# First attention of a two-layer model: four projections in one run, q and k six blocks ahead, scores a step early, running sums in float32r

## The chip, the cores and the metric

One core of one Trainium2 chip runs the whole program. The metric is device microseconds (us) from launch to end; lower is better. PE is TensorE, DVE VectorE, ACT ScalarE, POOL GpSimd, SP the queue that issues most DMAs.

## What is computed

The input is 64 sequences of 32 tokens with 256 features. Two layers follow, each of a conditioned linear map, an attention, a second conditioned map and a feed-forward net. The change touches only the first attention (16 heads, key and value width 128, 64 slots per head):

```python
q = _rope(hs @ Wq.T); k = _rope(hs @ Wk.T); v = hs @ Wv.T
s = clip(hs @ Ws1.T @ Ws2.T + bs2, -32, 32)
z = cumlogsumexp(s, over tokens); es = exp(s); enz = exp(-z)
A  = where(mask, q @ k.T * scale, 0)
ok = enz * (A @ es);  qv = softmax(ok, axis=-1)
W2 = where(mask, (qv * enz) @ es.T, 0)
o  = W2 @ v
o_n = o * rsqrt(mean(o*o) + EPS) * g_norm_weight
x  = x + (o_n * silu(hs @ Wg.T)) @ Wo.T
```

## The kernel before

`attention0` works in 64 steps. A step `i` is one block of 128 tokens (four sequences) and four heads; 16 blocks make a pass, and the four passes take the four groups of heads. `hs` and the projection weights are split in a high and a low float32r part, so each projection is six matmuls of 512 columns (two halves of the features, three products).

Each engine has its own program, written out by hand, and waits on semaphores. In a step, PE does:

- `x1(i)` and `x2(i)`: the two halves of a quarter of q or k (`quarter`), always over four blocks at once, so that four steps fill the q and k of the next four blocks. DVE multiplies each result by cosine and sine (`x1_by_cos`, `x1_by_sin`, `x2_by_both`), and POOL's `rotate` adds them.
- `proj_v(i+1)` into PSUM bank PJ0, which ACT's `v_out` copies out, and `proj_g(i+1)` into bank PJ1, which ACT's `g_t` (tanh) and DVE's `silu` read. `x1` and `x2` use the same two banks: `x1` waits for `v_out`, `x2` for `silu`.
- `slots(i+1)`: the slot logits, one float32r matmul; DVE's `clip`, then ACT's `s_e` makes `es`. `running(i+1)` multiplies `es` with a triangle of ones (float32, two passes) for the sums over tokens; DVE's `z` takes reciprocals (`enz`).
- `scores(i)` and `slot_scores(i)`, 32-wide tiles, with DVE's mask `am` between; then DVE's `ok` and its minimum `mn`, ACT's four exponentials `ex`, POOL's `exz`, and `turn_p(i)`, a transpose.
- `slot_weights(i)`, tiled; DVE's mask `wm`; `values(i-1)`, tiled; ACT's `square`, DVE's `norm_sum` and `gated`, POOL's `norm` (`rstd`, then `og`); `turn_og(i-1)`, transposes; ACT's `ogT_out`; `heads_out(i-2)`, four float32 matmuls (eight passes in the records); DVE's `y_out` adds to `xres`.

POOL also makes the low half of the next weights (`split`). The last four steps have no `x1` and `x2`. The file then goes on to stages that the change leaves alone.

Of the kernel before, what the change touches and what calls it, by code (L numbers as in the profile page):

```python
# [38 lines left out]
def attention0(nc, k, xres, x, cond, wcond, w_slices, wo, ws1, ws2b, ucol, gnorm, rope_cos, rope_sin, maskA, mask01, mask01_own):  # L39

    with ExitStack() as ctx:
# [23 lines left out]
        cosb = sb("cosb", [P, TOK])  # L65
        sinb = sb("sinb", [P, TOK])
# [13 lines left out]
        es = sb("es", [P, SW])  # L80
        enz = sb("enz", [P, SW])
# [16 lines left out]
        ogT_s = sb("ogT_s", [P, QW])  # L98
# [12 lines left out]
        products = [(t1c[:, :], t1s[:, :], t2c[:, :], t2s[:, :]), (gs[:, 1, :], og[:, :], sq[:, :], ogT_s[:, :])]  # L111
# [26 lines left out]
        TURNS = QUAD * (STEPS // QUAD)  # L138

# [20 lines left out]
        s_clip, s_exp, z_rec = sem("s_clip"), sem("s_exp"), sem("z_rec")  # L160
        a_mm, a_mask = sem("a_mm"), sem("a_mask")
# [44 lines left out]
        def _(pool):  # L206
# [37 lines left out]
            for j in range(QUAD):  # L244
                rotate(j)
# [11 lines left out]
            for i in range(STEPS):  # L257
                if i >= 1:
                    norm(i - 1)
                pool.wait_ge(ok_exp, HQ * (i + 1))  # L260
                pool.wait_ge(pT_tr, i)
                pool.tensor_tensor(exz[:, :], ex[:, :], enz[:, :], ALU.mult).then_inc(p_z, 1)
                if QUAD + i < TURNS:
                    rotate(QUAD + i)
                if LEAD + i < STEPS:
# [5 lines left out]
            norm(LAST)  # L271

        @block.tensor
        def _(pe):
# [51 lines left out]
            def x2(i, part):  # L326
                j = QUAD + i
                if j < TURNS:
                    if part.start == 0:
                        pe.wait_ge(g_silu, i + 1)  # L330
                    quarter(j, 1, x2_mm, part)

            def proj_v(i, part):
                if part.start == 0:
                    pe.wait_ge(x1_sin, min(QUAD + i, TURNS))
                    pe.wait_ge(v_ev, i)
                    pe.wait_ge(w_second, i // G * G + 1)
# [44 lines left out]
            def slot_scores(i):  # L382
                pe.wait_ge(a_mask, i + 1)
                pe.wait_ge(ok_z, i)
                for h in range(HQ):
# [11 lines left out]
            def heads_out(i):  # L397

                pe.wait_ge(ogT_ev, i + 1)
                pe.wait_ge(a_mask, min(i + 3, STEPS))  # L400
                pe.wait_ge(wo_scaled, i // G + 1)
                for h in range(HQ):
                    m = pe.matmul(AW[:, 2 * P:2 * P + D], ogT_s[:, h * P:(h + 1) * P], w_o[:, i // G % 2, h, :],  # L403
                                  start=(h == 0), stop=(h == HQ - 1))
                m.then_inc(y_mm, 1)
# [5 lines left out]
            def slot_weights(i):  # L411
                pe.wait_ge(pT_ev, i + 1)
                pe.wait_ge(esT_ev, i + 1)
                pe.wait_ge(y_add, i - 1) if i >= 2 else None
# [28 lines left out]
            for j in range(2, QUAD):  # L443
# [7 lines left out]
            proj_v(0, A)  # L451
            proj_g(0, A)
            pe.wait_ge(ld, 16 * LOADS)
            running(0)
            turn_es(0)
            for i in range(STEPS):
                more = i < LAST
                if i >= 1:
# [26 lines left out]
        def _(act):  # L485
# [53 lines left out]
            v_out(0)  # L539
            g_t(0)  # L540
            esT_out(0)
            split(G)
            def square(i):
# [4 lines left out]
            def ogT_out(i):  # L548
                act.wait_ge(y_mm, i)
                copy(ogT_s[:, :], TB[:, :], ogT_tr, i + 1, ogT_ev)  # L550

            for i in range(STEPS):
                more = i < LAST
                if i >= 1:
                    square(i - 1)
                if LEAD + i < STEPS:
                    split(LEAD + i)
# [6 lines left out]
                if more:  # L564
                    s_e(i + 1)
                act.wait_ge(w2_mm, i)
                copy(pT_s[:, :], TA[:, 0:SW], pT_tr, i + 1, pT_ev)
                if i >= 1:
                    ogT_out(i - 1)
                if more:  # L570
                    v_out(i + 1)
                    esT_out(i + 1)
                    g_t(i + 1)
            square(LAST)
# [3 lines left out]
        def _(dve):  # L578
# [20 lines left out]

            def x1_by_cos(j):  # L600
                dve.wait_ge(x1_mm, j + 1)
                dve.wait_ge(qk_add, j if j >= QUAD else max(j - 1, 0))
                dve.tensor_tensor(products_of(j)[0][:, :], banks_of(j)[0][:, :], cosb[:, :], ALU.mult).then_inc(x1_cos, 1)

            def x1_by_sin(j):
                dve.tensor_tensor(products_of(j)[1][:, :], banks_of(j)[0][:, :], sinb[:, :], ALU.mult).then_inc(x1_sin, 1)

            def x2_by_both(j):
                dve.wait_ge(x2_mm, j + 1)
                dve.tensor_tensor(products_of(j)[2][:, :], banks_of(j)[1][:, :], cosb[:, :], ALU.mult).then_inc(x2_cos, 1)  # L610
# [43 lines left out]
            for j in range(QUAD):  # L654
# [9 lines left out]
            for i in range(STEPS):  # L664
                j, more = QUAD + i, i < LAST
                silu(i)
                if i >= 1:
                    gated(i - 1)
                dve.wait_ge(a_mm, i + 1)
                dve.wait_ge(ok_mm, i)  # L670
                dve.tensor_tensor(by_pairs(am), both, for_heads(mA), ALU.mult).then_inc(a_mask, 1)
                if i >= 1:
                    norm_sum(i - 1)
                dve.wait_ge(ok_mm, i + 1)
                dve.wait_ge(z_rec, 2 * i + 2)
                dve.wait_ge(ok_exp, HQ * i)
                dve.scalar_tensor_tensor(out=ok[:, :], in0=OE[:, 0:SW], scalar=-1.0, in1=enz[:, :],
                                         op0=ALU.mult, op1=ALU.mult).then_inc(ok_z, 1)
                dve.wait_ge(ok_z, i + 1)
                dve.tensor_reduce(mn[:, :], heads(ok[:, :]), AX.X, ALU.min).then_inc(ok_min, 1)  # L680
                if more:
                    clip(i + 1)
# [3 lines left out]
                if i >= 2:  # L686
                    y_out(i - 2)
                dve.wait_ge(ok_exp, HQ * (i + 1))
                dve.tensor_reduce(sm[:, :], heads(ex[:, :]), AX.X, ALU.add).then_inc(p_sum, 1)
                dve.wait_ge(p_sum, i + 1)  # L690
                dve.scalar_tensor_tensor(out=sme[:, :], in0=sm[:, :], scalar=RMS_EPS, in1=sm[:, :],
                                         op0=ALU.mult, op1=ALU.mult).then_inc(p_eps, 1)
                if j < TURNS:
                    x2_by_both(j)
                if more:
                    z(i + 1, 0)
                    z(i + 1, 1)
                dve.wait_ge(w2_mm, i + 1)
                dve.wait_ge(o_mm, i)
# [1371 lines left out]
```

## Time and profile before

| | |
|---|---|
| median of three runs | 1491.48 us (1489.26 to 1494.16) |
| the profiled execution, its own time | 1494.37 us |
| its span, first to last instruction | 1492.5 us |
| busy: PE, DVE, ACT, POOL | 1361.8, 918.0, 507.1, 514.6 us |
| first attention, first to last mask `wm` | 67.0 to 805.7 us |
| the same, number of steps | 64 |
| mean granted TensorE clock | 0.968 |

The span is the profiled execution's own; the profiler's times of matmuls are modelled at their end, so a matmul's cost in a stream is read from the distance between two starts, not from its length.

### The profile page before, as it was taken

To read this page: it belongs to the slowest core of one execution; us is meant where nothing else is said; L and a number is where in the kernel's file an instruction comes from. 1 tells how busy PE (TensorE), PEld (TensorE's weight loads), DVE (VectorE), ACT (ScalarE), POOL (GpSimd) and SP (SyncE) were. 2 spreads that over 40 slices of the span, in tenths; PEclk is the share of its full clock that TensorE was granted. 3 is DMA by queue.
4 is the path that set the end of the run, shared out by engine and by line. 5 is a ranking of instruction groups with operands and counts; after the bars stand their busy time and mean duration, and the time that the engine had idled before them with its cause. 6 is when DMAs were issued, how large, how long until landed. Compare 5 with 4: busy or idle time off the path is not lost. (4 is left out here: it accounts for less than half of the span.)

```text
span 1492.5 us, 46698 instructions
## 1 busy us (share of the span) xinstructions
PE 1361.8 (91%) x19926; PEld 1060.2 (71%) x19926; DVE 918.0 (62%) x1825; ACT 507.1 (34%) x1123; POOL 514.6 (34%) x544
## 2 busy tenths in 40 slices
PE   2999999999999999999996598999999689997996
PEld 2677777777777777777764486777777567775664
DVE  2777777777777777777764465242433335665886
ACT  2344443444443444333342313132322222222332
POOL 0655545555544555544432212221212111122111
PEclk9999999999999999999999699999999879997998
DMA  6000000000001000000000510000000540000620
GB/s 200 9 13 13 14 16 13 27 13 13 13 16 28 13 13 13 3 2 3 2 2 2 201 52 1 0 0 0 0 1 0 167 121 1 0 0 3 197 66 22
DMA packets 33414, 47.57 MB, mean 32 GB/s; under 512 B 6718, under 2 KB 22296, under 8 KB 32728
## 3 DMA queue, kind: packets, MB, share of 16 engines
q1 hardware_dynamic: 31048, 42.69, 9.2%
q8 instruction: 133, 2.18, 0.6%
q10 hardware_dynamic: 2112, 2.10, 0.5%
q14 instruction: 41, 0.34, 0.1%
q0 software_dynamic: 80, 0.26, 0.1%
HBM read 42.68 MB, written 2.36 MB: 30 GB/s over the span
## 5 line engine op out<-in xcount | busy, mean ns | idle before, releaser
L233 POOL TENSOR_TENSOR rstd<-mse,mhalf 128x4 f32<-128x4 f32 x64 | 65.1, 1017 | 238.5 <-DVE mse L651 238.5
L563 ACT ACTIVATE ex<-ok,mn 128x64 f32<-128x64 f32 x256 | 68.2, 337 | 193.7 <-DVE mn L680 193.7
L403 PE MATMUL AW_TA<-w_o,ogT_s 128*128 128x256 f32 x512 | 129.0, 395 | 0.7 <-ACT ogT_s L488 0.7
L822 POOL TENSOR_TENSOR hT_lo<-h,hT_hi 128x512 fp32r<-128x512 f32 x44 | 56.8, 1292 | 192.8 <-ACT hT_hi L995 192.8
L228 POOL TENSOR_TENSOR turned<-t1c,t2s 128x512 f32<-128x512 f32 x62 | 79.8, 1287 | 117.5 <-DVE t2s L611 117.5
L626 DVE SCALAR_TENSOR_TENSOR gs<-gs,PJ 128x512 f32<-128x512 f32 x64 | 44.0, 687 | 122.5 <-ACT gs L504 122.5
L622 DVE RECIPROCAL enz<-SC 128x128 f32<-128x128 f32 x128 | 112.6, 921 | 4.7 <-PE SC L354 4.7
L303 PE MATMUL PJ<-hs_hi,w_hi 128*128 128x512 f32 x248 | 115.2, 464 | 0.0
L1058 DVE SCALAR_TENSOR_TENSOR t<-th,m 128x512 f32<-128x512 f32 (+1 forms) x56 | 38.4, 685 | 121.3 <-ACT th L1000 93.5
L314 PE MATMUL PJ<-w_hi,hs_hi 128*128 128x512 f32 x256 | 111.7, 436 | 0.0
L403 PEld LDWEIGHTS AW_TA<-w_o,ogT_s 128*128 128x128 f32 x512 | 93.0, 191 | 17.2 <-ACT ogT_s L488 1.0
L314 PE MATMUL PJ<-w_hi,hs_lo 128*128 128x512 f32 x256 | 100.2, 391 | 0.0
L314 PE MATMUL PJ<-w_lo,hs_hi 128*128 128x512 f32 x256 | 100.0, 391 | 0.0
L303 PE MATMUL PJ<-hs_hi,w_lo 128*128 128x512 f32 x248 | 98.2, 396 | 0.0
L303 PE MATMUL PJ<-hs_lo,w_hi 128*128 128x512 f32 x248 | 96.8, 390 | 0.0
L229 POOL TENSOR_TENSOR turned<-t2c,t1s 128x512 f32<-128x512 f32 x62 | 79.9, 1289 | 0.0
L995 ACT ACTIVATE hT_hi<-h 128x512 fp32r<-128x512 f32 (+1 forms) x56 | 35.4, 632 | 124.4 <-DVE h L1064 124.4
L432 PE MATMUL OO<-v_s,wm 32*32 32x128 f32 x2048 | 68.9, 271 | 0.5 <-DVE wm L700 0.5
L236 POOL TENSOR_TENSOR og<-og,rstd 128x512 f32<-128x512 f32 x64 | 66.5, 1039 | 5.0
L432 PEld LDWEIGHTS OO<-v_s,wm 32*32 32x32 f32 x2048 | 51.7, 104 | 22.8 <-issue 22.2
L1254 POOL TENSOR_TENSOR r<-qk,raw 128x128 f32<-128x128 f32 x16 | 7.4, 463 | 152.6 <-DVE qk L1483 152.6
L637 DVE TENSOR_TENSOR og<-OO,gs 128x512 f32<-128x512 f32 x64 | 44.3, 692 | 25.5 <-ACT sq L546 25.5
(378 smaller groups left out, 3440.6 us busy)
## 6 DMA issues: line engine op xcount, KB each, us to landing
we_ring<-in_we SPq DMA_DIRECT2D x64, 256.0 KB, 3.0
w_raw<-in_w_slices SPq DMA_DIRECT2D x48, 128.0 KB, 2.1
turned<-in_w_slices ACTq DMA_DIRECT2D x4, 512.0 KB, 7.6
xres<-in_x SPq DMA_DIRECT2D x2, 1024.0 KB, 14.3
out_rows<-xres SPq DMA_DIRECT2D x16, 128.0 KB, 1.7
w1r<-in_w1i SPq DMA_DIRECT2D x1, 1408.0 KB, 6.7
w_s<-in_w SPq DMA_DIRECT2D x2, 682.0 KB
w_o<-in_wo SPq DMA_DIRECT2D x1, 1024.0 KB, 5.4
```

What stands on the lines that cost most here:

```text
L228: pool.tensor_tensor(to[:, 0, :], x1c[:, :], x2s[:, :], ALU.subtract)
L229: pool.tensor_tensor(to[:, 1, :], x2c[:, :], x1s[:, :], ALU.add).then_inc(qk_add, 1)
L233: pool.tensor_tensor(rstd[:, :], mse[:, :], mhalf[:, :], ALU.pow).then_inc(o_rstd, 1)
L236: pool.tensor_tensor(heads(og[:, :]), heads(og[:, :]), rstd[:, :].unsqueeze(2).to_broadcast([P, HQ, DK]), ALU.mult).then_inc(o_norm, 1)
L303: m = pe.matmul(banks_of(j)[half][:, :], w[:, slot, a:a + P], h[:, c, toks], start=(n == 0), stop=(n == len(terms) - 1))
L314: m = pe.matmul(bank[:, :], h[:, c, toks], w[:, slot, a:a + QW], start=(n == 0), stop=(n == len(terms) - 1))
L403: m = pe.matmul(AW[:, 2 * P:2 * P + D], ogT_s[:, h * P:(h + 1) * P], w_o[:, i // G % 2, h, :], start=(h == 0), stop=(h == HQ - 1))
L432: m = pe.matmul(OO[toks, h * P:(h + 1) * P], wm[toks, h, :], v_s[toks, i % 2, h * P:(h + 1) * P], start=True, stop=True, tile_position=(b ...
L563: act.activation(ex[:, cols], ok[:, cols], ACT.Exp, scale=-1.0, bias=mn[:, h:h + 1]).then_inc(ok_exp, 1)
L622: dve.reciprocal(enz[:, cols], SC[:, SW:2 * SW][:, cols]).then_inc(z_rec, 1)
L637: dve.tensor_tensor(og[:, :], OO[:, :], gs[:, i % 2, :], ALU.mult).then_inc(o_gate, 1)
L822: eng.tensor_tensor(hT[1][s, m % 2, :], h[s, m % 2, :], hT[0][s, m % 2, :].bitcast(F32), ALU.subtract).then_inc(second, 1)
```

## The change

All in `attention0`:

- The four projections of a step stand in one run on PE: `slots`, `proj_v`, `proj_g`, `x1`, `running`, `x2`.
- `x1` and `x2` work on block quarter `j = i + 6` (was `i + 4`); five quarters stand ahead of the loop, and the last six steps have none.
- `slots`, `clip`, `s_e`, `running` and the first `z` are two steps ahead; `scores`, the mask `am`, `slot_scores`, `ok`, `mn` and `ex` one step ahead.
- `running` multiplies in float32r: `m01` is copied once to `m01_r`; ACT makes a rounded `es_hi` by a second exponential, POOL's `slots_low` makes `es_lo = es - es_hi`, and PE does two 256-column matmuls.
- `heads_out` is cut in two halves that stand around `turn_og` and `slot_weights`, writes to another bank (OE), and `ogT_s` has two buffers.
- The cosine and sine tables are 32 columns wide instead of 512 and are read repeated.
- On DVE, `norm_sum` stands ahead of `gated`, and the last `y_out`s come after them.

```diff
-        cosb = sb("cosb", [P, TOK])
+        cosb = sb("cosb", [P, T])
...
+        FIRST = QUAD + 1
...
+            def slots_low(i):
+                pool.wait_ge(s_first, i + 1)
+                pool.wait_ge(cum_mm, i)
+                pool.tensor_tensor(es_lo[:, :], es[:, :], es_hi[:, :].bitcast(F32), ALU.subtract).then_inc(s_second, 1)
...
             def running(i):
-                pe.wait_ge(s_exp, i + 1)
-                pe.matmul(SC[:, SW:2 * SW], m01[:, :], es[:, :], start=True, stop=True).then_inc(cum_mm, 1)
+                pe.wait_ge(s_second, i + 1)
+                pe.matmul(SC[:, SW:2 * SW], m01_r[:, :], es_hi[:, :], start=True, stop=False)
+                pe.matmul(SC[:, SW:2 * SW], m01_r[:, :], es_lo[:, :], start=False, stop=True).then_inc(cum_mm, 1)
-            for i in range(STEPS):
-                more = i < LAST
-                if i >= 1:
-                    values(i - 1)
-                scores(i)
-                x1(i)
-                if more:
-                    slots(i + 1)
-                slot_scores(i)
+            for i in range(-1, STEPS):
+                now, one, two = i >= 0, i + 1 < STEPS, i + 2 < STEPS
+                if now:
+                    turn_p(i)
                 if i >= 2:
-                    heads_out(i - 2)
-                x2(i, A)
-                turn_p(i)
-                if more:
-                    running(i + 1)
+                    heads_out(i - 2, (0, 2))
                 if i >= 1:
                     turn_og(i - 1)
-                if more:
+                if now:
+                    slot_weights(i)
+                if i >= 2:
+                    heads_out(i - 2, (2, HQ))
+                if one:
+                    turn_es(i + 1)
+                    scores(i + 1)
+                if now:
+                    values(i)
+                if one:
+                    slot_scores(i + 1)
+                if two:
+                    slots(i + 2)
+                if one:
                     proj_v(i + 1, A)
-                slot_weights(i)
-                if more:
-                    turn_es(i + 1)
                     proj_g(i + 1, A)
-            values(LAST)
+                x1(i + 1 + FIRST)
+                if two:
+                    running(i + 2)
+                x2(i + 1 + FIRST)
...
+            def s_high(i):
+                act.wait_ge(cum_mm, i)
+                act.activation(es_hi[:, :], sclip[:, :], ACT.Exp).then_inc(s_first, 1)
+            act.activation(m01_r[:, :], m01[:, :], ACT.Copy).then_inc(m01_in, 1)
```

PE before, in the middle of a step: `slots`, `slot_scores`, `heads_out`, `x2`, `turn_p`. `PJ` is the two projection banks, `SC` slots and running sums, `AW_TA` scores, weights and transposes.

```order
L349 MATMUL SC<-w_s,uT 128x256 [waits z_rec]
L388 MATMUL OE<-es,am 32x64 [waits ok_z,a_mask]
L388 MATMUL OE<-es,am 32x64 x15
L403 MATMUL AW_TA<-w_o,ogT_s 128x256 [waits wo_scaled,a_mask,ogT_ev]
L403 MATMUL AW_TA<-w_o,ogT_s 128x256 x3
L303 MATMUL PJ<-hs_hi,w_hi 128x512 [waits g_silu]
L303 MATMUL PJ<-hs_lo,w_hi 128x512
L303 MATMUL PJ<-hs_hi,w_lo 128x512
L303 MATMUL PJ<-hs_hi,w_hi 128x512
L303 MATMUL PJ<-hs_lo,w_hi 128x512
L303 MATMUL PJ<-hs_hi,w_lo 128x512
L358 MATMUL AW_TA<-ident,exz 128x128 [waits p_z]
```

PE now, the same place of the loop: the end of `proj_g`, then `x1`, `running` and `x2` without a change of kind between them.

```order
L329 MATMUL PJ<-w_lo,hs_hi 128x512
L318 MATMUL PJ<-hs_hi,w_hi 128x512 [waits v_ev]
L318 MATMUL PJ<-hs_lo,w_hi 128x512
L318 MATMUL PJ<-hs_hi,w_lo 128x512
L318 MATMUL PJ<-hs_hi,w_hi 128x512
L318 MATMUL PJ<-hs_lo,w_hi 128x512
L318 MATMUL PJ<-hs_hi,w_lo 128x512
L366 MATMUL SC<-es_hi,m_r 128x256 [waits s_second]
L367 MATMUL SC<-es_lo,m_r 128x256
L318 MATMUL PJ<-hs_hi,w_hi 128x512 [waits g_silu]
L318 MATMUL PJ<-hs_lo,w_hi 128x512
L318 MATMUL PJ<-hs_hi,w_lo 128x512
```

What moved: `x1` and `x2` follow the other two projections, and `running` is two short matmuls inside the run, with a wait for `s_second`, which POOL gives.

PE before, the tiled work: `values` of one step (L432) and `scores` of the next (L377) follow a projection, and `x1` follows them; `slot_scores` and `slot_weights` stand elsewhere, each alone.

```order
L432 MATMUL OO<-v_s,wm 32x128 [waits o_gate,o_sq,v_ev,w2_mask]
L432 MATMUL OO<-v_s,wm 32x128 x15
L377 MATMUL AW_TA<-turned 32x32 [waits w2_mask,qk_add]
L377 MATMUL AW_TA<-turned 32x32 x31
L303 MATMUL PJ<-hs_hi,w_hi 128x512 [waits v_ev]
L303 MATMUL PJ<-hs_lo,w_hi 128x512
L303 MATMUL PJ<-hs_hi,w_lo 128x512
L303 MATMUL PJ<-hs_hi,w_hi 128x512
L303 MATMUL PJ<-hs_lo,w_hi 128x512
L303 MATMUL PJ<-hs_hi,w_lo 128x512
```

PE now: the tiled groups stand together, but for `slot_weights`, which parts the two halves of `heads_out` (L419).

```order
L436 MATMUL AW_TA<-pT_s,esT_s 32x32 [waits esT_ev,pT_ev]
L436 MATMUL AW_TA<-pT_s,esT_s 32x32 x15
L419 MATMUL OE<-w_o,ogT_s 128x256 x2
L371 MATMUL TB<-ident,es 128x128 [waits ogT_ev,s_exp]
L371 MATMUL TB<-ident,es 128x128
L390 MATMUL AW_TA<-turned 32x32 [waits w2_mask,qk_add]
L390 MATMUL AW_TA<-turned 32x32 x31
L448 MATMUL OO<-v_s,wm 32x128 [waits o_gate,o_sq,v_ev,w2_mask]
L448 MATMUL OO<-v_s,wm 32x128 x15
L402 MATMUL OE<-es,am 32x64 [waits y_add,ok_z,a_mask]
L402 MATMUL OE<-es,am 32x64 x15
L361 MATMUL SC<-w_s,uT 128x256 [waits z_rec]
```

What moved: `scores`, `values` and `slot_scores` are one stretch of tiled work, and the run of projections begins behind them with `slots` (L361).

ACT before, one step.

```order
L546 ACTIVATE sq<-OO 128x512 [waits o_ms,o_mm]
L510 ACTIVATE w_hi<-w_raw 128x256 [waits w_next_odd]
L563 ACTIVATE ex<-ok,mn 128x64 [waits p_sum,p_z,ok_min]
L563 ACTIVATE ex<-ok,mn 128x64 x3
L495 ACTIVATE es<-sclip 128x256 [waits s_clip]
L488 ACTIVATE pT_s<-AW_TA 128x256 [waits pT_tr,w2_mm]
L488 ACTIVATE ogT_s<-TB 128x512 [waits ogT_tr,y_mm]
L488 ACTIVATE v_s<-PJ 128x512 [waits v_mm]
L488 ACTIVATE esT_s<-TB 128x256 [waits esT_tr,w2_mm]
L504 ACTIVATE gs<-PJ 128x512 [waits o_gate,g_mm]
```

ACT now, one step: `v_s` and `gs` stand behind the exponentials, with the new `es_hi` between them.

```order
L581 ACTIVATE sq<-OO 128x512 [waits o_ms,o_mm]
L572 ACTIVATE ex<-ok,mn 128x64 [waits p_sum,p_z,ok_min]
L572 ACTIVATE ex<-ok,mn 128x64 x3
L514 ACTIVATE es<-sclip 128x256 [waits s_second,s_clip]
L506 ACTIVATE v_s<-PJ 128x512 [waits v_mm]
L518 ACTIVATE es_hi<-sclip 128x256 [waits cum_mm]
L527 ACTIVATE gs<-PJ 128x512 [waits o_gate,g_mm]
L506 ACTIVATE pT_s<-AW_TA 128x256 [waits pT_tr,w2_mm]
L506 ACTIVATE ogT_s<-TB 128x512 [waits ogT_tr,y_mm]
L506 ACTIVATE esT_s<-TB 128x256 [waits esT_tr,w2_mm]
```

What moved: `x1` and `x2` on PE now wait for `v_s` and `gs` within the same run of projections, and `s_first` goes to POOL between the two.

## Rows read from the trace of the kernel before

**Rows 1.** Busy us of PE, PEld, DVE, ACT, POOL, then granted clock, four steps.
```profile
349.00:396.00 47.00, 47.00 (x813) 36.95 (x812) 34.66 (x73) 19.35 (x48) 23.91 (x25) 1.00 0.05 14
```

**Rows 2.** Timeline of PE, one step: start us, length us, instruction.
```profile
400.25 0.50 PE L303 MATMUL PJ<-hs_hi,w_hi 128*128 128x512 f32 x1
400.58 0.40 PE L303 MATMUL PJ<-hs_lo,w_hi 128*128 128x512 f32 x1
...
401.74 0.28 PE L349 MATMUL SC<-w_s,uT 96*128 96x256 f32 x1
401.95 0.65 PE L388 MATMUL OE<-es,am 32*32 32x64 f32 x32
402.53 1.99 PE L403 MATMUL AW_TA<-w_o,ogT_s 128*128 128x256 f32 x8
404.18 0.58 PE L303 MATMUL PJ<-hs_hi,w_hi 128*128 128x512 f32 x1
...
405.75 0.38 PE L358 MATMUL AW_TA<-ident,exz 128*128 128x128 f32 x2
405.97 0.60 PE L354 MATMUL SC<-es,m 128*128 128x256 f32 x2
406.40 0.60 PE L358 MATMUL TB<-ident,og 128*128 128x128 f32 x4
406.76 0.48 PE L314 MATMUL PJ<-w_hi,hs_hi 128*128 128x512 f32 x1
...
408.32 0.35 PE L420 MATMUL AW_TA<-pT_s,esT_s 64*32 64x32 f32 x32
...
408.80 0.48 PE L314 MATMUL PJ<-w_hi,hs_hi 128*128 128x512 f32 x1
...
410.35 1.08 PE L432 MATMUL OO<-v_s,wm 32*32 32x128 f32 x32
411.36 0.76 PE L377 MATMUL AW_TA<-turned 64*32 64x32 f32 x64
412.05 0.50 PE L303 MATMUL PJ<-hs_hi,w_hi 128*128 128x512 f32 x1
```

**Rows 3.** The mask `wm`, once in each of 64 steps: first and last start.
```profile
L700 DVE TENSOR_TENSOR wm<-AW_TA,m_own x64: 228/292/293, 67.0 to 805.7; 128x128 f32<-128x128 f32 x64
```

**Rows 4.** Timeline of the other engines in the same step; in brackets the wait before.
```profile
402.14 1.02 POOL L233 TENSOR_TENSOR rstd<-mse,mhalf 128x4 f32<-128x4 f32 x1 [2.23 <-DVE mse L651]
402.67 0.42 DVE L677 SCALAR_TENSOR_TENSOR ok<-OE,enz 128x256 f32<-128x256 f32 x1 [0.61 <-PE OE L388]
403.24 1.04 POOL L236 TENSOR_TENSOR og<-og,rstd 128x512 f32<-128x512 f32 x1
403.58 1.07 ACT L563 ACTIVATE ex<-ok,mn 128x64 f32<-128x64 f32 x4 [2.99 <-DVE mn L680]
404.55 0.40 ACT L495 ACTIVATE es<-sclip 128x256 f32<-128x256 f32 x1
404.73 0.74 POOL L262 TENSOR_TENSOR exz<-ex,enz 128x256 f32<-128x256 f32 x1 [0.45 <-ACT ex L563]
408.43 0.60 ACT L488 ACTIVATE v_s<-PJ 128x512 f32<-128x512 f32 x1 [0.73 <-PE PJ L314]
410.46 0.60 ACT L504 ACTIVATE gs<-PJ 128x512 f32<-128x512 f32 x1 [0.94 <-PE PJ L314]
411.09 0.69 DVE L626 SCALAR_TENSOR_TENSOR gs<-gs,PJ 128x512 f32<-128x512 f32 x1 [1.94 <-ACT gs L504]
```

**Rows 5.** Timeline of PE ahead of the loop: `slots`, then a projection.
```profile
53.60 0.28 PE L349 MATMUL SC<-w_s,uT 96*128 96x256 f32 x1
53.78 0.50 PE L314 MATMUL PJ<-w_hi,hs_hi 128*128 128x512 f32 x1
```

**Rows 6.** Timeline: a step without `x1` and `x2`, and the end of the attention.
```profile
770.93 0.44 PE L358 MATMUL AW_TA<-ident,exz 128*128 128x128 f32 x2 [1.12 <-POOL exz L262]
...
809.13 0.42 DVE L631 TENSOR_TENSOR xres<-AW_TA,xres 128x256 f32<-128x256 f32 x1 [3.09 <-PE AW_TA L403]
```

More of the change, by code:

```diff
@@ L80, in attention0 @@
         es = sb("es", [P, SW])
+        m01_r = sb("m01_r", [P, P], F32R)
+        es_hi = sb("es_hi", [P, SW], F32R)
+        es_lo = sb("es_lo", [P, SW], F32R)
         enz = sb("enz", [P, SW])
@@ L256, in _ @@
             scale_out(1)
-            for i in range(STEPS):
-                if i >= 1:
[L259 to L265, printed above, removed]
+            for i in range(-1, STEPS):
+                j, now, one, two = i + 1 + FIRST, i >= 0, i + 1 < STEPS, i + 2 < STEPS
+                if one:
+                    pool.wait_ge(ok_exp, HQ * (i + 2))
+                    pool.wait_ge(pT_tr, i + 1)
+                    pool.tensor_tensor(exz[:, :], ex[:, :], enz[:, :], ALU.mult).then_inc(p_z, 1)
+                if two:
+                    slots_low(i + 2)
+                if now:
+                    norm(i)
+                if j < TURNS:
+                    rotate(j)
+                if now and LEAD + i < STEPS:
                     split(LEAD + i)
@@ L395, in turn_og, with heads_out @@
                 turn(TB, og, HQ, ogT_tr)
[L397 to L403, printed above, removed]
+            def heads_out(i, part=(0, HQ)):
+                if part[0] == 0:
+                    pe.wait_ge(ogT_ev, i + 1)
+                    pe.wait_ge(y_add, i)
+                    pe.wait_ge(ok_z, min(i + 3, STEPS))
+                    pe.wait_ge(wo_scaled, i // G + 1)
+                for h in range(*part):
+                    m = pe.matmul(OE[:, SW:SW + D], ogT_s[:, i % 2, h * P:(h + 1) * P], w_o[:, i // G % 2, h, :],
                                   start=(h == 0), stop=(h == HQ - 1))
-                m.then_inc(y_mm, 1)
+                if part[1] == HQ:
+                    m.then_inc(y_mm, 1)
             def turn_p(i):
@@ L537, in _, with exps @@
                 act.activation(uT[:, n * 512:(n + 1) * 512], bank[0:RW, :], ACT.Identity, bias=u_col[:, 0:1]).then_inc(u_high, 1)
+            act.activation(m01_r[:, :], m01[:, :], ACT.Copy).then_inc(m01_in, 1)
             s_e(0)
-            v_out(0)
-            g_t(0)
-            esT_out(0)
+            s_high(0)
             split(G)
-            def square(i):
-                act.wait_ge(o_mm, i + 1)
-                act.wait_ge(o_ms, i)
-                act.activation(sq[:, :], OO[:, :], ACT.Square).then_inc(o_sq, 1)
[L548 to L557, printed above, removed]
+            def exps(i):
                 act.wait_ge(ok_min, i + 1)
@@ L563, in _, with pT_out, square, ogT_out @@
                     act.activation(ex[:, cols], ok[:, cols], ACT.Exp, scale=-1.0, bias=mn[:, h:h + 1]).then_inc(ok_exp, 1)
-                if more:
-                    s_e(i + 1)
+            def pT_out(i):
                 act.wait_ge(w2_mm, i)
                 copy(pT_s[:, :], TA[:, 0:SW], pT_tr, i + 1, pT_ev)
+            def square(i):
+                act.wait_ge(o_mm, i + 1)
+                act.wait_ge(o_ms, i)
+                act.activation(sq[:, :], OO[:, :], ACT.Square).then_inc(o_sq, 1)
+            def ogT_out(i):
+                act.wait_ge(y_mm, i - 1) if i >= 2 else None
+                copy(ogT_s[:, i % 2, :], TB[:, :], ogT_tr, i + 1, ogT_ev)
+            for i in range(-1, STEPS):
+                now, one, two = i >= 0, i + 1 < STEPS, i + 2 < STEPS
+                if now:
+                    pT_out(i)
                 if i >= 1:
                     ogT_out(i - 1)
-                if more:
+                if one:
+                    esT_out(i + 1)
+                if now:
+                    if LEAD + i < STEPS:
+                        split(LEAD + i)
+                    square(i)
+                if one:
+                    exps(i + 1)
+                if two:
+                    s_e(i + 2)
+                if one:
                     v_out(i + 1)
-                    esT_out(i + 1)
+                if two:
+                    s_high(i + 2)
+                if one:
                     g_t(i + 1)
-            square(LAST)
             ogT_out(LAST)
@@ L663, in _ @@
             z(0, 1)
[L664 to L682, printed above, removed]
+            for i in range(-1, STEPS):
+                j, now, one, two = i + 1 + FIRST, i >= 0, i + 1 < STEPS, i + 2 < STEPS
+                if now:
+                    mask_weights(i)
+                if now and one:
+                    z(i + 1, 1)
+                if i >= 2:
+                    y_out(i - 2)
+                if one:
+                    mask_scores(i + 1)
+                    slot_max(i + 1)
+                if two:
+                    clip(i + 2)
+                if now:
+                    norm_sum(i)
+                    gated(i)
+                if one:
+                    slot_sum(i + 1)
+                    silu(i + 1)
                 if j < TURNS:
@@ L685, in _ @@
                     x1_by_sin(j)
[L686 to L692, printed above, removed]
+                if two:
+                    z(i + 2, 0)
                 if j < TURNS:
                     x2_by_both(j)
[L695 to L699, printed above, removed]
-                dve.tensor_tensor(by_pairs(wm), both, for_heads(m01_own), ALU.mult).then_inc(w2_mask, 1)
             y_out(LAST - 1)
-            gated(LAST)
-            norm_sum(LAST)
             y_out(LAST)
```

89 lines of the change are left out of this document (58 added, 31 removed).

## Prediction

> **What bounds the kernel now.** I read the windows first: in four steps of the first attention PE is busy 47.00 of 47.00 us at a granted clock of 1.00, DVE 34.66, POOL 23.91, ACT 19.35 [rows 1]. No wait of PE shows there, so a step lasts as long as PE's own list. Then the timeline of PE for one step, from one `x1` to the next: 412.05 - 400.25 = 11.80 us [rows 2]. The attention's masks run from 67.0 to 805.7 us, 738.7 us for 63 intervals, 11.73 each; the last four lack `x1` and `x2` [rows 3]. It is half of the time, and the only part that the change touches.
>
> The distances between starts give the price of each group [rows 2]: `x1` 1.49, `slots` 0.21, `slot_scores` 0.58, `heads_out` 1.65, `x2` 1.57, `turn_p` 0.22, `running` 0.43, `turn_og` 0.36, `proj_v` 1.56, `slot_weights` and the transposes of `es` together 0.48, `proj_g` 1.55, `values` 1.01, `scores` 0.69. The sum is 11.80. The reader is to see that a projection's first matmul costs more than the others: 400.58 - 400.25 = 0.33, then (401.74 - 400.58) / 5 = 0.232 each.
>
> **The run of projections.** The same matmuls cost before 1.49 + 0.21 + 1.57 + 1.56 + 1.55 + 0.43 = 6.81 us. Now: `slots`, which stands behind tiled work, 0.10 for that (0.33 less 0.232) and the 53.78 - 53.60 = 0.18 that it took between projections [rows 5]; then 0.33 + 23 x 0.232 = 5.67; then `running`. No row shows a float32r matmul of 256 columns beside its equals. Half of 0.232 is 0.12, an estimate by columns; the dear end is the 0.21 of `slots` [rows 2]. I take 0.12 twice, since nothing changes kind around them, and keep 0.42 in all as the other end. Sum 0.28 + 5.67 + 0.24 = 6.19: saved 0.62 a step.
>
> **What the other groups lose.** `heads_out` and `turn_og` now hand over to float32 or tiled work. At the 0.43 / 2 = 0.215 of a 256-column float32 pass, eight passes are 1.72 (before 1.65), and at the 0.11 of `turn_p`'s transposes, four are 0.44 (before 0.36), two 0.22, which with some 0.29 for `slot_weights` is 0.51 (before 0.48). That is +0.18. Two new changes from full to tiled work, `turn_og` to `slot_weights` and the transposes of `es` to `scores`, cost between nothing and 0.10 each (the 0.10 above is the nearest row); I take 0.07, so +0.14. Net a step: 11.80 - 0.62 + 0.18 + 0.14 = 11.50. Bounds: 11.26 with free changes and free `slots` entry; 11.74 with the dear `running` and the changes at 0.10.
>
> **A rule beside it.** PE changed between full and tiled work, or between tile shapes, seven times a step and now does five times. The Trainium skill, TensorEngine Tiling (Array Packing), section Key Properties, says that changing the tiling mode drains the TensorE. The extra 0.10 of `x1`'s first matmul behind tiled work agrees [rows 2]; by the rule alone two changes fewer at 0.10 and the cheaper `running` (0.19) would make 11.41. The sum above goes by the rows of each group.
>
> **Does PE still find its inputs?** That is the risk: `x1` and `x2` had most of a step for their banks to clear, now they wait within the run. Time from the start of `slots`, which now stands where `heads_out` stood, just behind `slot_scores` (402.53) [rows 2, 4]. `ex` begins at 403.58, so +1.05, `es` at +2.02, ends +2.42. `v_s` was before ready 408.43 - 406.76 = 1.67 behind `proj_v`, here +1.95, but ACT is free only at +2.42: ends +3.02. PE wants `x1` at 0.28 + 0.33 + 11 x 0.232 = +3.16. `es_hi` follows in 0.4, +3.42; POOL has done `exz` (+2.20 to +2.94) and needs 0.74: `es_lo` at +4.2, wanted at +4.55. `gs` is ready 410.46 - 408.80 = 1.66 behind `proj_g` (+1.77): +3.43; `silu` 411.09 - 410.46 = 0.63 later, and 0.69 long: +4.75. PE wants `x2` at +4.79. So each arrives, the last by 0.04 us. I count these waits as nothing, up to 0.1 in the upper bound's neighbourhood. `ex` to `turn_p`: `exz` ends +2.94 against +6.2, ample. `rstd` starts after `es_lo`, +4.2, `og` follows by 1.10 and takes 1.04 [rows 4]: +6.4, while `turn_og` is wanted at 6.19 + 0.22 + 0.86 = +7.3. DVE is the next engine: 34.66 / 4 = 8.7 busy a step before and about the same work after (tables read repeated have the same element count), under 11.5.
>
> The one `exp` more on ACT (0.40) and the subtraction on POOL (0.74) are hidden: ACT had 19.35 and POOL 23.91 busy in 47. Without that cover each would add its own length to the wait before `running`. The narrower tables cut two loads ahead of the loop; PE does not wait for them at that time, so nothing.
>
> **Ends.** Ahead of the loop: one more quarter, 12 x 0.232 = 2.8 from 53.60, so PE is at 56.4; DVE's products to 57.9; clip 0.4, two exponentials 0.7, `es_lo` 0.8 and hand-overs: 60.0. Then reciprocals, mask, `slot_scores` to 63.2, and the first `wm` 8.0 later, 71.2 instead of 67.0: +4.2. The first two intervals lack `heads_out`: 10.6 + 11.1 = 21.7. Then 56 intervals of 11.50 = 644.0. Five steps without `x1` and `x2`: POOL decides, `es_lo` +4.1, `rstd` and `og` to +6.2, then `turn_og` to `slot_scores` 0.44 + 0.51 + 0.86 + 0.69 + 1.01 + 0.58 and the 0.14: 10.4; before, such a step waited too, 1.12 at `turn_p` [rows 6]. Four of them and a shorter last, 9.4: 51.0. From the old first mask on: 4.2 + 21.7 + 644.0 + 51.0 = 720.9 against 738.7, -17.8. At the end `gated` and `norm_sum` no longer stand behind a `y_out` that waited 3.09 [rows 6]; part of it they waited for `square` anyway: -2 (bounds 0 and -3). Sum -19.8.
>
> The sum is against the profiled execution, 1494.4 with a span of 1492.5, which gives 1474.6; that execution lies 2.9 over the median of the three, so on the median it is 1491.5 - 19.8 = **1471.7 us**.
>
> **Rivals.**
> - *Nothing but the run counts* (0.14): changes between kinds of float32 work are free, 11.26 a step, 56 x 0.24 = 13 less: 1458. For it: `turn_p` and `running` follow one another at the bare 0.11 and 0.215. Against: every group before tiled work paid.
> - *The ring through `silu` shows* (0.15): `x2` waits 0.1 to 0.3 us, 11.74: 1485. For it: a margin of 0.04 us worked out from five rows. Against: only a wait beyond the 0.10 that a first matmul loses anyhow is felt twice.
> - *Slower* (0.11): the same ring, one mechanism. If `v_s` on ACT ends later than +3.02, because ACT takes `ex`, `es` and `v_s` further apart than 402.67 to 404.55 shows or because a busy PSUM bank holds it, then `x1`, `es_hi`, `gs`, `silu` and `x2` shift together. From 0.35 us a step on, the gain is gone; at 0.5 it is 56 x 0.5 = 28 more: 1500. Against it: the same ACT instructions had these distances in each step before.
> - *No change to tell* (0.08): the groups give back in new places what the run saves, 11.80 again, about 1488.
> - My forecast, 1464 to 1480: 0.52.
>
> **Numbers.** A difference under 0.3% (4.5 us) cannot be told from none. Range 1457 to 1487: it holds the forecast, the first two rivals and leaves 2 in 10 outside. Faster: 0.52 + 0.14 + 0.15 = 0.81, less some 0.02 of the ring's upper part: 0.79. Same: 0.10. Slower: 0.11.
>
> **What would show it.** Right: the distance between two `wm` is 11.4 to 11.6, from `slots` to `turn_p` 6.2; `running`'s two matmuls 0.24; no wait of PE on `silu`, `v_s` or `es_lo`; first `wm` near 71. Wrong: an idle time of PE before `x2` or before `running` above 0.1 us; DVE busy all the time, with `wm` late and `scores` waiting for it; more than 0.2 lost where `heads_out` is cut; or a changed later stage, which I leave at its time.

## The result and the profile after

The median is 1483.02 us (1482.42 to 1484.12), against 1490.47 of the kernel before in the same comparison: a ratio of 0.9944 (0.9929 to 0.9960), faster by 7.45 us. I had forecast 1471.7. In the two profiled executions the gap is 1494.37 - 1484.12 = 10.25 us, since that of before lay 3.9 over its median and that of after 1.1; the places below are read from these two.

| stretch, us | before | forecast | after |
|---|---|---|---|
| first mask `wm` | 67.0 | 71.2 | 72.6 |
| first two intervals | 23.2 | 21.7 | 21.9 |
| 56 full steps | 660.9 | 644.0 | 650.3 |
| last five | 54.6 | 51.0 | 53.1 |
| last `wm` to the span's end | 686.8 | 684.8 | 684.4 |

The shortfall is 1.4 + 0.2 + 6.3 + 2.1 - 0.4 = 9.6 us. The mask answers to [rows 3] (count, shortest, median and longest in ns, first and last start):

```profile
L718 DVE TENSOR_TENSOR wm<-AW_TA,m_own x64: 280/292/293, 72.6 to 797.9; 128x128 f32<-128x128 f32 x64
```

The same window as [rows 1], now over four steps and a part:

```profile
349.00:396.00 47.00, 45.80 (x814) 37.45 (x812) 34.90 (x73) 19.93 (x52) 26.71 (x28) 1.00 0.05 14
```

PE is no longer busy all the time: 1.2 us are missing, at an unchanged clock. An undisturbed step, PE's timeline from `slots` to `slots`, which answers to [rows 2]:

```profile
388.64 0.39 PE L361 MATMUL SC<-w_s,uT 96*128 96x256 f32 x1
388.87 0.40 PE L329 MATMUL PJ<-w_hi,hs_hi 128*128 128x512 f32 x1
...
391.61 0.48 PE L318 MATMUL PJ<-hs_hi,w_hi 128*128 128x512 f32 x1
391.93 0.40 PE L318 MATMUL PJ<-hs_lo,w_hi 128*128 128x512 f32 x1
...
393.08 0.28 PE L366 MATMUL SC<-es_hi,m_r 128*128 128x256 f32 x1
393.20 0.28 PE L367 MATMUL SC<-es_lo,m_r 128*128 128x256 f32 x1
393.32 0.39 PE L318 MATMUL PJ<-hs_hi,w_hi 128*128 128x512 f32 x1
...
394.69 0.38 PE L371 MATMUL AW_TA<-ident,exz 128*128 128x128 f32 x2
394.90 1.03 PE L419 MATMUL OE<-w_o,ogT_s 128*128 128x256 f32 x4
395.77 0.60 PE L371 MATMUL TB<-ident,og 128*128 128x128 f32 x4
396.30 0.35 PE L436 MATMUL AW_TA<-pT_s,esT_s 64*32 64x32 f32 x32
396.58 1.13 PE L419 MATMUL OE<-w_o,ogT_s 128*128 128x256 f32 x4
397.55 0.38 PE L371 MATMUL TB<-ident,es 128*128 128x128 f32 x2
397.86 0.76 PE L390 MATMUL AW_TA<-turned 64*32 64x32 f32 x64
398.58 1.07 PE L448 MATMUL OO<-v_s,wm 32*32 32x128 f32 x32
399.45 0.65 PE L402 MATMUL OE<-es,am 32*32 32x64 f32 x32
400.03 0.39 PE L361 MATMUL SC<-w_s,uT 96*128 96x256 f32 x1
```

400.03 - 388.64 = 11.39 us, under the forecast's 11.50. `running` takes 0.24 as forecast. So an ordinary step doesn't explain the shortfall: of the 56 distances between masks the median is 11.43, but ten are 12.0 to 12.8, and these ten together are 10.5 us longer than ten medians. In such a step (PE's timeline):

```profile
374.35 1.08 PE L448 MATMUL OO<-v_s,wm 32*32 32x128 f32 x32
375.22 0.49 PE L402 MATMUL OE<-es,am 32*32 32x64 f32 x19
376.88 0.41 PE L402 MATMUL OE<-es,am 32*32 32x64 f32 x13 [1.16 <-issue]
377.22 0.39 PE L361 MATMUL SC<-w_s,uT 96*128 96x256 f32 x1
```

PE stops in the middle of `slot_scores`, between two equal matmuls, and waits for nothing that has a semaphore ("issue"). The waits of PE over all full steps, 90 to 740 us (total, times, longest), name no other engine:

```profile
PE OE L402 <- issue: 7.2, 8, 1.2
PE SC L361 <- issue: 0.9, 1, 0.9
PE PJ L329 <- issue: 0.5, 1, 0.5
```

**What the stops share.** The page counts the packets of the instruction queue:

```profile
q8 instruction: 133, 2.18, 0.6%
```

2.18 MB in 133 packets is 16.4 KB each. That is 256 instructions if one has 64 bytes, which no trace here shows; the count bears the 256 out. I counted PE's instructions (weight loads, matmuls and separate waits) up to each stop. Every stop stands at the same place of a block of 256, instruction 194 of my count. A step has 417 or 418 instructions, so this place moves through the step. Placing it in each step, I read how long PE took from the start of `scores` to the start of `x1`, by how far the block start lay behind the start of `slot_scores`:

```
block start, instructions behind the start of slot_scores | us
 2 to 22   | 5.12 to 5.17
28, 32, 38 | 6.13, 6.49, 6.53
41, 48, 54 | 6.59, 6.23, 5.96
58, 64, 70 | 5.80, 6.13, 5.83
74 to 252  | 5.12 to 5.30
```

`scores`, `values` and `slot_scores` are 128 + 64 + 64 = 256 instructions and pass in 400.03 - 397.86 = 2.2 us. The kernel before had at most 192 tiled instructions in a row, never took less than 3.5 us for any 256 instructions in its full steps, and none of its 56 intervals was long (median 11.80, all excess together 0.1 us). Outside the full steps, where a step has fewer long matmuls, a stop can stand in `values` too (at 790.24, below), at the same instruction 194. **My theory:** where a new block is needed 28 to 70 instructions into `slot_scores`, it has been used up faster than the next one arrives. **Rivals:** the stop comes from the work (a PSUM bank, a data-dependent wait that the profile can't name), or from tiled matmuls following one another, wherever the block starts.

### The profile page after: what moved, and what is told of

Read it like the earlier page. It is cut to its first block and busy times, and to the rows that moved or that the text cites. A ratio compares the mean times of both kernels' runs of the same rounds, so it can differ in the third digit from the quotient of the medians.

```text
span 1482.3 us, 47081 instructions
## 1 busy us (share of the span) xinstructions
PE 1342.1 (91%) x19926; PEld 1069.0 (72%) x19926; DVE 921.8 (62%) x1825; ACT 517.4 (35%) x1188; POOL 556.5 (38%) x608
## 3 DMA queue, kind: packets, MB, share of 16 engines
q8 instruction: 133, 2.18, 0.6%
## 5 line engine op out<-in xcount | busy, mean ns | idle before, releaser
L419 PE MATMUL OE<-w_o,ogT_s 128*128 128x256 f32 x512 | 137.9, 392 | 0.7 <-ACT ogT_s L506 0.7
L661 DVE RECIPROCAL enz<-SC 128x128 f32<-128x128 f32 x128 | 121.3, 949 | 2.9 <-PE SC L367 2.5
L274 POOL TENSOR_TENSOR exz<-ex,enz 128x256 f32<-128x256 f32 x64 | 47.4, 740 | 181.2 <-ACT ex L572 181.2
L318 PE MATMUL PJ<-hs_hi,w_hi 128*128 128x512 f32 x248 | 102.6, 414 | 0.0
L329 PE MATMUL PJ<-w_hi,hs_hi 128*128 128x512 f32 x256 | 100.8, 394 | 0.0
L419 PEld LDWEIGHTS OE<-w_o,ogT_s 128*128 128x128 f32 x512 | 87.1, 190 | 10.4 <-ACT ogT_s L506 1.0
L506 ACT ACTIVATE pT_s<-AW_TA 128x256 f32<-128x256 f32 x64 | 24.6, 384 | 167.7 <-PE AW_TA L371 167.7
L697 DVE SCALAR_TENSOR_TENSOR ok<-OE,enz 128x256 f32<-128x256 f32 x64 | 27.2, 425 | 89.8 <-PE OE L402 89.8
L1048 ACT ACTIVATE hT_hi<-h 128x512 fp32r<-128x512 f32 (+1 forms) x56 | 35.4, 632 | 124.6 <-DVE h L1117 124.6
```

Of the source, the lines that this page charges most:

```text
L318: m = pe.matmul(banks_of(j)[half][:, :], w[:, slot, a:a + P], h[:, c, toks], start=(n == 0), stop=(n == len(terms) - 1))
L329: m = pe.matmul(bank[:, :], h[:, c, toks], w[:, slot, a:a + QW], start=(n == 0), stop=(n == len(terms) - 1))
L419: m = pe.matmul(OE[:, SW:SW + D], ogT_s[:, i % 2, h * P:(h + 1) * P], w_o[:, i // G % 2, h, :], start=(h == 0), stop=(h == HQ - 1))
L661: dve.reciprocal(enz[:, cols], SC[:, SW:2 * SW][:, cols]).then_inc(z_rec, 1)
```

## The experiments

**Padding, in lumps.** Waits that have long been fulfilled are added to PE, so that a step has 448 instructions and the place repeats every four steps. `pad_good` and `pad_bad` differ only in the waits ahead of the loop, 58 or none, two making one instruction.

```diff
+            def filler(n):
+                for _ in range(n):
+                    pe.wait_ge(ld, 16 * LOADS)
...
+            filler(58)
...
+                filler(EXTRA(i, 0))
                 x1(i + 1 + FIRST)
...
+                    filler(EXTRA(i, 1))
                     running(i + 2)
...
+                filler(EXTRA(i, 2))
                 x2(i + 1 + FIRST)
```

> The changed kernel with idle wait instructions on PE inside each step's run of projections, so that every full step has exactly 448 PE instructions (before 417 or 418), and 29 more ahead of the loop. Nothing else is changed. Theory A (instruction blocks): PE's instructions arrive in blocks of 256, and a block that begins 28 to 70 instructions behind the start of slot_scores comes up to 1.4 us late, since scores, values and slot_scores use up 256 instructions in about 2.2 us. With 448 a step the block starts stand at 18 of each 64, never in that window: no such stall in the 56 full intervals, each about 11.40, so about 10 us less than the changed kernel, near 1473. Theory B (data: a late weight, a semaphore of another engine): the long steps stay where they are, about 1483 or more by the added instructions.

> The same kernel as pad_good without the 29 idle instructions ahead of the loop; each step is the same. Theory A: block starts stand 47 instructions behind slot_scores in every fourth step, inside the window, and 1.1 to 1.4 us are lost there: 14 steps, 15 to 20 us more than pad_good, near 1490, with long intervals at a distance of exactly four steps. Theory B: no difference from pad_good.

`pad_good` took 1519.0 us (ratio 1.0208, 1.0183 to 1.0233), `pad_bad` 1533.65 (1.0305, 1.0278 to 1.0333). PE's waits in the full steps, first of `pad_good`:

```profile
PE PJ L318 <- issue: 23.7, 53, 0.5
```

and of `pad_bad`:

```profile
PE PJ L318 <- issue: 24.8, 52, 0.8
PE OE L402 <- issue: 9.9, 12, 1.1
```

The place of the block start alone is worth 1533.65 - 1519.0 = 14.65 us: `pad_bad` has intervals of 12.9 to 13.6 at every fourth step but one, `pad_good` has a median of 12.25 and none that is long. But both are slower than before: lumps of ten instructions that do nothing cost 0.8 us a step (12.25 against 11.43). That is a price of the tool, not of the change, and it had to go.

**Padding, spread.** The same count, two or four waits (one or two instructions) at a time between 512-column matmuls; `even_bad` has `filler(18)` ahead of the loop in place of 74.

```diff
+            spread = [0]
...
+                    if n:
+                        filler(spread[0] * (2 if n in (2, 3, 4) else 1))
...
+            filler(74)
...
+                spread[0] = 2 if 1 <= i <= 57 else 0
```

> As pad_good, 448 PE instructions in each full step, but the idle waits are spread singly over the run of projections instead of in three lumps of ten, and those ahead of the loop stand where PE waits anyway. Theory A (a block of 256 instructions that begins 28 to 70 behind slot_scores is late): block starts stand 19 behind it, modulo 64, so no long interval; if single idle instructions hide behind the 0.23 us of a matmul, intervals are the 11.40 of the changed kernel without its long ones, and the time is about 10 us below it: 1473. Rival: each idle instruction costs PE's queue its own time wherever it stands; then intervals are near the 12.25 of pad_good, and the time 1510 to 1518.

> even_good with 18 idle waits ahead of the loop instead of 74 (28 PE instructions fewer); every step is the same. Theory A: block starts stand 47 instructions behind slot_scores in every fourth step, in the window where the changed kernel lost 1.1 to 1.4 us. 14 such steps: 15 to 20 us more than even_good, 1486 to 1491, so no faster than the kernel before. Rival (the idle waits as such help, by holding PE back in the run): no difference from even_good, 1471.

`even_good` took 1470.77 us (0.9854, 0.9840 to 0.9869), `even_bad` 1485.64 (0.9967, 0.9956 to 0.9977). PE's waits in the full steps, `even_good`:

```profile
PE PJ L339 <- issue: 0.2, 1, 0.2
```

and `even_bad`:

```profile
PE OE L412 <- issue: 11.0, 14, 1.2
```

PE's timeline in `even_bad`, one of the fourteen:

```profile
377.06 0.53 PE L412 MATMUL OE<-es,am 32*32 32x64 f32 x23
378.06 0.32 PE L412 MATMUL OE<-es,am 32*32 32x64 f32 x9 [0.47 <-issue]
```

Same work, same order, same number of instructions a step; 28 instructions more or fewer ahead of the loop are 14.9 us, and 14.3 us in the 56 intervals of the two traces (654.3 for 640.0). The data and the banks are the same in both and tiled matmuls follow one another in both, so both rivals fall. Against the changed kernel, `even_good` is 12.25 us faster, with 56 intervals of 640.0 us in sum for 650.3; the rest is in the first two intervals (21.2 for 21.9), in the last steps (52.6 for 53.1), in the first mask and in the two profiles' distance from their medians. The Trainium skill, Runtime: NRT & Kernel Launch, section Instruction fetch mechanics, tells of instructions that are fetched in blocks while the engine runs on; what it calls mostly hidden was hidden in the kernel before and shows here.

**The packets themselves.** The traces hold the time of each packet of the instruction queue. In the changed kernel, between the block start at 372.21 and the stop that ended at 376.88, there is one, which ran from 374.08 to 375.55 (DMA of the window 372.3:376.8):

```profile
q8 instruction: 1, 0.02, 2.0%
```

In the full steps of each trace in this table there are exactly as many packets as block starts, one for each in order. From the end of a block's packet to PE's first matmul of that block it takes, in us:

```
kernel      | stops | where PE stopped | all other blocks
before      |  0    | -                | 2.57 or more
after       | 10    | 1.30 to 1.50     | 1.50 or more
even_bad    | 14    | 1.23 to 1.56     | 1.81 or more
even_good   |  0    | -                | 1.52 or more
```

So PE never enters a block sooner than about 1.2 us behind the end of its packet, and each stop ends within 1.6 us of it: PE waits for the packet. It isn't a plain race between PE and one block, though. The block before the stop at 376.88 took PE 3.3 us without the stop of 1.4; the one before 306.35 took 2.97 and there was none. The packet of the first began 1.87 us behind the block start before it, that of the second 0.32 ahead of it. What sets a packet's start is open.

**Parting the tiled stretch.** If the dense stretch matters, half of `heads_out` between `scores` and `values` should end the stops without any padding. (On DVE, the mask of the scores then stands ahead of `y_out`; the diff shows PE alone.)

```diff
-                if i >= 2:
-                    heads_out(i - 2, (2, HQ))
                 if one:
                     turn_es(i + 1)
                     scores(i + 1)
+                if i >= 2:
+                    heads_out(i - 2, (2, HQ))
                 if now:
                     values(i)
```

> The changed kernel without idle instructions, but the second half of heads_out stands between scores and values (and DVE masks the scores before it adds y). 128 tiled instructions, then 0.9 us of heads_out, then 128. Theory A: the stalls of about 1 us vanish or shrink, -10 us; one change between full and tiled work more, 0.1 to 0.2 a step, +6 to +11: within 4 us of the changed kernel, and the interval without a stall 11.5 to 11.6. Theory B: the long intervals stay, 6 to 11 us slower.

It took 1518.46 us (1.0196, 1.0176 to 1.0215). PE's waits in the full steps:

```profile
PE TB L371 <- ACT ogT_s L506: 29.8, 54, 0.6
PE OE L402 <- issue: 0.5, 2, 0.3
```

The stops on issue fall from 8.6 us to 0.5, which speaks for the theory, though not cleanly: PE now also stands still just ahead of `scores`, which gives a packet time. I had expected the changed kernel's time within 4 us, and it is 35.4 us slower. The half of `heads_out` had covered `ogT_out`: `turn_es` writes to the bank that ACT is still reading, and now PE waits 0.55 us for it in each of 54 steps (29.8 / 54). An ordinary step is 12.15, 0.72 longer; I put the other 0.17 down to the two changes between full and tiled work more, at about 0.1 each, which nothing here parts.

**The price of `running`.** Back to one float32 matmul of `es` (`z` waits as before; the second exponential and the subtraction stay). `good_f32` does this in `pad_good`, `after_f32` in the changed kernel.

```diff
-                pe.matmul(SC[:, SW:2 * SW], m01_r[:, :], es_hi[:, :], start=True, stop=False)
-                pe.matmul(SC[:, SW:2 * SW], m01_r[:, :], es_lo[:, :], start=False, stop=True).then_inc(cum_mm, 1)
+                pe.matmul(SC[:, SW:2 * SW], m01[:, :], es[:, :], start=True, stop=True).then_inc(cum_mm, 1)
```

> pad_good with running back to one float32 matmul of es (two passes), the high and low parts still made by ACT and POOL. The same number of PE instructions. The forecast's term: 0.43 instead of 0.24 us, 0.19 more a step, and with two changes of kind inside the run up to 0.2 more: 62 x 0.19 = 12 us to 24 us slower than pad_good. Rival: float32 among float32r costs nothing beyond its passes and part is hidden: under 8 us.

> The changed kernel with running back to one float32 matmul of es in two passes, at the same place in the run, the high and low parts still made. The number of PE instructions is the same, so block starts are the same. The forecast's term: 0.43 instead of 0.24 us a step, 0.19 x 62 = 12 us slower than the changed kernel, near 1495; with changes of kind at 0.1 each up to 1505. Rival: the float32 pass hides something else and costs under 5 us.

`good_f32` took 1518.43 us (1.0196, 1.0176 to 1.0215), no different from `pad_good`: the lump of empty instructions before `x2` hid what was to be measured. PE's idle time there on issue fell from 23.7 us to 12.5, which is 0.20 for each of 56 steps. `after_f32` took 1493.96 (1.0022, 1.0013 to 1.0032), 10.9 more than the changed kernel (7.7 by the two spans; its trace has less of the stops, 4.8 us for 8.6). Its ordinary intervals are 11.60 to 11.63 for 11.39 to 11.44, so 0.20 a step. PE's timeline:

```profile
396.81 0.59 PE L366 MATMUL SC<-es,m 128*128 128x256 f32 x2
397.05 0.58 PE L318 MATMUL PJ<-hs_hi,w_hi 128*128 128x512 f32 x1
397.47 0.40 PE L318 MATMUL PJ<-hs_lo,w_hi 128*128 128x512 f32 x1
```

From the start of the first float32 pass to the start of the second matmul behind the passes it is 397.47 - 396.81 = 0.66, which is two passes of 0.215 and one matmul of 0.23; with the float32r pair it is 0.47. So what float32r saves is the 0.19 that the forecast had, the longer passes themselves, and no change of kind. The split of the 0.66 in the record, 0.24 and then 0.42, is no measure: a matmul behind a float32 pass is recorded as started about 0.03 behind it. The kernel before has the same behind `heads_out`: `x2`'s first matmul is recorded at 404.18 [rows 2], 0.03 behind the eighth pass, and the next comes 0.41 later:

```profile
404.59 0.39 PE L303 MATMUL PJ<-hs_lo,w_hi 128*128 128x512 f32 x1
```

**The start.** `slots(0)` moved ahead of the fifth quarter, DVE's `clip(0)` after the fourth.

```diff
             for j in range(FIRST):
+                if j == QUAD:
+                    slots(0)
                 quarter(j)
-            slots(0)
```

(The diff leaves the two waits of `slots(0)` out; the loop is written in short.)

> The changed kernel with slots(0) and clip(0) ahead of the fifth quarter in the part before the loop, so that running(0) finds its input sooner. PE idled 3.24 us there and its granted clock was 0.50 from 60 to 66 us. If that idle time is what costs, it falls to about 2 us and the first wm comes 1.3 us sooner (2.5 if the clock stays up): 1480 to 1482. Rival: the wait moves to the mask or to slot_scores and nothing changes.

> even_good and early together. If both hold, the fastest version: 1471. If single idle instructions are not free, 1510 to 1517.

`early` took 1481.0 us (0.9931, 0.9918 to 0.9943): 2.0 under the changed kernel, too little for this measurement to tell from none. The wait ahead of the first `running` shrank from 3.24 us (below) to 1.88, so `running` began 0.73 sooner:

```profile
59.06 0.36 PE L366 MATMUL SC<-es_hi,m_r 128*128 128x256 f32 x1 [1.88 <-POOL es_lo L252]
```

But PE then waited 1.10 us for the mask `am`, where it had waited 0.76, and the granted clock still fell to 0.50 and stayed there a us longer (0.50 for 66 to 67 us, where the changed kernel has 0.82). The first `wm` came at 72.55, no sooner than the 72.59 of the changed kernel. `early_even`, the same edit in `even_good`, took 1468.21 (0.9845, 0.9832 to 0.9857), the fastest kernel of this study, 14.8 under the changed one. Its first `wm` came at 71.6 for 72.3 in `even_good`; the other 2 us between their medians can't be told from the spread of either (1467.6 to 1473.34 for `even_good`).

## Why the prediction was right and wrong

**Direction and mechanism: right.** The run gives back what it was said to, and in an ordinary step PE stays the bound. Start distances of an ordinary step, by the forecast's own terms:

| term | forecast | after |
|---|---|---|
| `slots` to `turn_p` | 6.19 | 6.04 |
| `turn_p` | 0.22 | 0.22 |
| `heads_out`, both halves | 1.72 | 1.83 |
| `turn_og`, `slot_weights`, `es` transposes, with the 0.14 | 1.09 | 1.13 |
| `scores`, `values`, `slot_scores` | 2.28 | 2.17 |
| sum | 11.50 | 11.39 |

The changes between full and tiled work do cost, some 0.1 each, on the matmul beside the change: the half of `heads_out` behind `slot_weights` takes 0.97, the other 0.87, and the last transposes ahead of `slot_weights` and of `scores` take 0.20 where the others take 0.11. My 0.07 for those two was near, and the 0.10 in `heads_out` I had left out. Against that, I had charged the entry from tiled work twice, on `slots` and on the first projection behind it: `slots` took 0.22, not 0.28 (0.12 for its columns and 0.10 for the change), and that projection's first matmul 0.24, not 0.33. The tiled groups cost 0.11 less side by side. The step by the rule on tiling modes, 11.41, came closer than my sum; since my errors nearly cancel, this is no proof of it.

**The ring: nearly right.** I gave `x1` a margin of 0.14 us, `x2` 0.04. ACT and POOL in the step from 400.03:

```profile
402.36 0.57 ACT L506 ACTIVATE v_s<-PJ 128x512 f32<-128x512 f32 x1
402.84 0.40 ACT L518 ACTIVATE es_hi<-sclip 128x256 fp32r<-128x256 f32 x1
403.18 0.60 ACT L527 ACTIVATE gs<-PJ 128x512 f32<-128x512 f32 x1
403.31 0.74 POOL L252 TENSOR_TENSOR es_lo<-es,es_hi 128x256 fp32r<-128x256 f32 x1 [0.35 <-ACT es_hi L518]
```

`v_s` ends at 402.93, which is +2.90 for the +3.02 of the forecast, but PE is at `x1` at +2.95 for its +3.16, so the margin is 0.05. PE's timeline:

```profile
402.98 0.50 PE L318 MATMUL PJ<-hs_hi,w_hi 128*128 128x512 f32 x1
403.32 0.40 PE L318 MATMUL PJ<-hs_lo,w_hi 128*128 128x512 f32 x1
```

The first matmul takes 0.34 instead of 0.23, though no kind changes there; the idle column shows nothing. In 53 full steps of this trace it starts under 0.12 us behind the end of `v_s` and takes 0.28 to 0.34. Where `v_s` came early, it doesn't, ACT first:

```profile
414.22 0.60 ACT L506 ACTIVATE v_s<-PJ 128x512 f32<-128x512 f32 x1 [0.38 <-PE PJ L329]
```

and PE:

```profile
415.39 0.39 PE L318 MATMUL PJ<-hs_hi,w_hi 128*128 128x512 f32 x1
415.61 0.39 PE L318 MATMUL PJ<-hs_lo,w_hi 128*128 128x512 f32 x1
```

Over this kernel, `even_good` and `early_even` there are 6 full steps in which `v_s` was over 0.3 us ahead, all at 0.22 to 0.24, and some 160 others, all at 0.27 to 0.34. So it looks as if `x1` waits about 0.1 us for `v_s` in each step, 5 us in all, for which my sum had nothing. I didn't try to end this wait, so it is argued, not shown. (In the kernel before, the 0.33 of `x1` was another thing, the entry from tiled work: its `v_s` had ended at 409.03 [rows 4], 3 us ahead of `x1` at 412.05.) `x2`, the narrower margin on paper, takes its 0.23: `silu` ends at +4.49 and PE is there at +4.68, so it is in time, and neither ring rival came about (the steps have 0.1 us of it, not the 0.35 from which the gain is gone).

**What failed: "a step lasts as long as PE's own list", 56 x 11.50 with no term for the supply of instructions.** Ten steps paid 0.6 to 1.4 us, 10.5 in all. That the place of the block start is the cause is shown by `even_good` against `even_bad`, and that PE there waits for the packet of its instructions by the packets' own times. That the dense stretch is needed is borne out by the kernel before and, less cleanly, by `heads_between`; why a packet starts as late as it does stays open. With the stops taken away in `even_good`, 1470.77 us is within 1 us of the 1471.7 forecast, and that is in part luck, since the errors above and below partly cancel.

**The ends.** The first mask came 5.6 us later, not 4.2. PE stood idle for 3.24 us, and the granted clock then was at 0.50, the lower level, from 60 to 66 us. PE's timeline:

```profile
59.79 0.55 PE L366 MATMUL SC<-es_hi,m_r 128*128 128x256 f32 x1 [3.24 <-POOL es_lo L252]
```

The windows behind it (columns as in [rows 1]):

```profile
60.00:63.00 3.00, 2.24 (x86) 1.78 (x90) 1.91 (x3) 0.38 (x1) 3.00 (x4) 0.50 0.03 5
63.00:66.00 3.00, 3.00 (x30) 2.43 (x23) 1.46 (x4) 1.37 (x5) 2.22 (x3) 0.50 0.18 46
66.00:70.00 4.00, 4.00 (x19) 3.29 (x18) 1.80 (x5) 1.50 (x3) 1.23 (x2) 0.95 0.00 0
```

I had forecast the idle time (PE at work again at 60.0) but priced all behind it at the full clock. Of the last five steps three took 10.5 to 10.6 us, near the forecast's 10.4; one of 11.18 had a stop, and the last took 10.32 where I had 9.4. PE's timeline there shows the two waits that I named and the stop that I did not:

```profile
784.35 0.39 PE L366 MATMUL SC<-es_hi,m_r 128*128 128x256 f32 x1 [0.88 <-POOL es_lo L252]
...
786.52 0.63 PE L371 MATMUL TB<-ident,og 128*128 128x128 f32 x4 [0.59 <-POOL og L241]
...
790.24 0.96 PE L448 MATMUL OO<-v_s,wm 32*32 32x128 f32 x28 [0.60 <-issue]
```

Behind the last mask 2.4 us were gained where I had 2, in part by chance: from there to the last `y_out` it was 9.2 us for 12.4, 3.1 gained, and the later stages, which are the same, took 0.7 more. Those stages vary from trace to trace (669 to 675 us over all runs here).

## What to carry to other kernels

Where many small tiled matmuls are put side by side, count the engine's instructions, not only its microseconds: here a stretch as long as a block of 256 ran in about 2 us, its place against the block starts decided, and a single trace showed good and bad steps of one program. Look at the spread of the step time, not at one step; and where a stop has "issue" as its cause between two equal instructions, shift the program by a few instructions before looking for a dependency. A margin of a tenth of a us between a copy and the matmul that waits for its bank may be no margin: look at the distance to the next matmul, since the idle column stays empty. And read the price of a float32 matmul over its neighbour as well, since the record gives part of its time to the next one.

## What the runs showed of the hardware

- Ten stops of 0.6 to 1.4 us at block starts, in a stretch of 256 tiled instructions in 2.2 us; none at 192 in a row. PE never entered a block sooner than 1.23 us behind the end of its 16.4 KB packet, and all stops (10 in the changed kernel, 14 in `even_bad`) ended 1.23 to 1.56 us behind it.
- Waits that are long fulfilled cost nothing that shows when they stand two or four at a time between 512-column matmuls (median step 11.41 in `even_good`, 11.43 without them), but 0.8 us a step in three lumps of ten.
- Two float32r matmuls of 256 columns inside a float32r run are 0.24 us; two float32 passes in the same place cost 0.20 more, as much as their columns: 0.66 with the next matmul for 0.47.
- A change between full and tiled work cost PE about 0.1 us in either direction (transposes 0.20 for 0.11, a `heads_out` pass 0.32 for 0.22).
- A first matmul right behind the end of the copy that it waits for took 0.27 to 0.34 us to the next start where 0.23 is ordinary; the timeline shows no idle time.
- Behind 3.24 us of idle PE the granted clock was 0.50 for 6 us while PE was at work again; behind 1.88 us in `early` it fell too.
